# A graph network's edge loops: ring of 24 chunks, destination matrices four at a time, tables ordered by node

## What is computed

```
def _gine(x, src, dst, edge_attr, W1, b1, W2, b2, eW, eb, eps):
    e = edge_attr @ eW + eb
    m = jax.nn.relu(x[src] + e)
    agg = jax.ops.segment_sum(m, dst, num_segments=N)
    h = (1.0 + eps) * x + agg
    return jax.nn.relu(h @ W1 + b1) @ W2 + b2
...
h_all = jnp.einsum('nf,rof->rno', x, W).reshape(r, n, h, d)
h_src = h_all[edge_type, src]
h_dst = h_all[edge_type, dst]
scores = jnp.einsum('ehd,hd->eh', h_src, attn_src) + jnp.einsum('ehd,hd->eh', h_dst, attn_dst)
scores = jnp.where(scores > 0, scores, NEG_SLOPE * scores)
amax = jnp.maximum(jax.ops.segment_max(scores, dst, num_segments=n), 0.0)
w = jnp.exp(scores - amax[dst])
w = w / (jax.ops.segment_sum(w, dst, num_segments=n) + 1e-12)[dst]
out = jax.ops.segment_sum(h_src * w[..., None], dst, num_segments=n)
```

## Time and profile before

| what | value |
|---|---|
| time, median of 3 runs | 4963.34 us (4953.61 to 4967.11) |
| the profiled execution's own time, its span | 5003.4 us, 5001.7 us |
| granted TensorE clock, mean | 0.765 |
| message passes, by windows | 428 to 434 us each, four |
| between passes (layer network, normalisation) | some 70 us each |
| scores stage, attention pass | 500 us, 418 us |
| the rest after attention | 1539 us |

### The profile page before, as it was taken

How to read it: one execution, slowest core, us unless ns; L and a number is a source line. 1 busy time by engine, 2 the same in 40 slices (tenths; PEclk the granted TensorE clock), 3 DMA queues, 4 the chain that set the end, 5 groups by cost and what they waited for, 6 DMA issues and landing times. The chain is left out here.

```text
span 5001.7 us, 66979 instructions
## 1 busy us (share of the span) xinstructions
PE 2986.3 (60%) x16584; PEld 2451.0 (49%) x16585; DVE 2257.8 (45%) x6573; ACT 909.3 (18%) x2422; POOL 2091.8 (42%) x2246
## 2 busy tenths in 40 slices
PE   4566656665666566624366533554677937948392
PEld 3455545554555455514345421222666836947382
DVE  7655555554555455553322235666125441134213
ACT  1122222221222122201011101111120012310020
POOL 4355555556555655553454555663110011020212
PEclk8777877877778787766677755776788968979596
DMA  6522222222223222304221101222766718956494
GB/s 175 184 83 82 70 65 82 82 74 60 82 81 74 62 82 82 77 17 165 49 53 44 44 2 55 85 86 63 242 227 226 239 70 281 329 172 215 142 337 140
DMA packets 394658, 597.59 MB, mean 119 GB/s; under 512 B 105798, under 2 KB 279160, under 8 KB 394104
## 3 DMA queue, kind: packets, MB, share of 16 engines
q1 hardware_dynamic: 274744, 357.76, 21.9%
q0 software_dynamic: 97088, 214.27, 15.5%
q10 hardware_dynamic: 22656, 23.54, 1.4%
HBM read 499.63 MB, written 95.75 MB: 119 GB/s over the span
## 5 line engine op out<-in xcount | busy, mean ns | idle before, releaser
L790 POOL DMA_INDIRECT gine_got<-gine_table,src x1056 | 999.8, 947 | 769.9 <-ACT gine_msg L899 413.6
L886 PE MATMUL gine_p_sum<-gine_hot,gine_msg 128*128 128x128 f32 x4224 | 901.1, 350 | 609.7 <-DVE gine_hot L916 283.5
L886 PEld LDWEIGHTS gine_p_sum<-gine_hot,gine_msg 128*128 128x128 f32 x4224 | 760.2, 253 | 751.7 <-ACT gine_msg L899 538.0
L920 DVE TENSOR_TENSOR gine_got<-gine_got,gine_p_edge 128x256 f32<-128x256 f32 x1056 | 436.6, 413 | 669.1 <-remote 281.5
L899 ACT ACTIVATE gine_msg<-gine_got 128x256 f32<-128x256 f32 x1056 | 439.9, 417 | 1301.2 <-DVE gine_got L920 799.3
L927 DVE TENSOR_TENSOR stack_acc<-stack_acc,gine_p_sum 128x256 f32 x1056 | 434.7, 412 | 2.6
L480 POOL DMA_INDIRECT adjacency<-value,place x264 | 289.2, 1095 | 223.2 <-issue 77.1
L877 PE MATMUL gine_p_edge<-gine_w_a,attrs_t 128*128 128x256 bf16 x1056 | 351.7, 333 | 45.8 <-issue 45.8
L878 PE MATMUL gine_p_edge<-gine_w_b,attrs_t 128*128 128x256 bf16 x1056 | 350.3, 332 | 0.0
L916 DVE TENSOR_SCALAR gine_hot<-iota_free,dst 128x128 f32<-128x128 f32 x1056 | 310.6, 294 | 86.3 <-issue 42.7
L1366 PE MATMUL ffn_p_h<-ffn_xt,ffn_w 128*128 128x128 f32 x2864 | 345.9, 279 | 1.6 <-DMA ffn_w<-in_L_ffn_w 0.9
(11 more groups left out here) (402 smaller groups left out, 3537.6 us busy)
## 6 DMA issues: line engine op xcount, KB each, us to landing
gcn_a<-adjacency SPq DMA_DIRECT2D x270, 320.0 KB, 3.7
ffn_w<-in_L_ffn_W SPq DMA_DIRECT2D x74, 1024.0 KB
ffn_w<-in_L_ffn_w SPq DMA_DIRECT2D x60, 1024.0 KB, 6.3
ffn_w<-in_L_ffn_w SPq DMA_DIRECT2D x90, 512.0 KB
adjacency<-zero_row ACTq DMA_DIRECT2D x3, 7200.0 KB, 43.9
gine_got<-gine_table,src POOLq DMA_INDIRECT x1056
h_table<-score_rows SPq DMA_DIRECT2D x15, 1024.0 KB
adjacency<-zero_row SPq DMA_DIRECT2D x1, 7200.0 KB, 28.0
```

Of the source, the lines that this page charges most:

```text
L790: pool.indirect_dma_start(got[:, u, :], None, table, bass.IndirectOffsetOnAxis(ap=rows[:, c:c + 1], axis=0)).then_inc(gathered[u], 16)
L886: ins = nc.tensor.matmul(p_sum[u % 4][:, half * P:(half + 1) * P], msg[:, u % U, half * P:(half + 1) * P], hot[:, u % U, :], start=True, s ...
L920: nc.vector.tensor_tensor(got[:, u, :], got[:, u, :], p_edge[u % 4][:, 0:D], ALU.add).then_inc(summed, 1)
```

## The change

- `RING = 24` slots of `got` instead of 12. In the message passes the relu works in place in `got`, in attention the multiply and the tail copy too (the slot is 265 wide there), and `msg` is gone. A gather waits for the aggregation of chunk c-24.
- `HOTS = 12` destination matrices, made four at a time by one `tensor_tensor` of 128x512 (`destinations`).
- PE, ScalarE and VectorE are written out over all 264 chunks: waits compare with constants and slices are fixed. The tile register stays (`Tiles`, two banks of 12 registers, one load per 12 chunks). SP's raises are gone.
- The tables' rows are ordered `src * R + etype`: `src_table` is written by one DMA with 256 B pieces, a tile of `h_table` with 8 KB in one piece per partition where it was 8 pieces of 1 KB.

```diff
-            nc.vector.scalar_tensor_tensor(g.hrow[:, some], g.etype[:, some], float(NP), g.src[:, some], ALU.mult, ALU.add)
+            nc.vector.scalar_tensor_tensor(g.hrow[:, some], g.src[:, some], float(R), g.etype[:, some], ALU.mult, ALU.add)
...
+class Tiles:
+    def load(self, c):
+        if c % U == 0:
+            b = c // U % 2
+            self.eng.load(self.registers[b], self.g.chunk_tile[0:1, c:c + U])
+            self.now[b] = [self.eng.snap(r, min_val=0, max_val=T - 1) for r in self.registers[b]]
+def gather_rows(nc, pool, rows, table, got, gathered, used):
+    for c in range(EC):
+        if c >= RING:
+            pool.wait_ge(used, c - RING + 1)
+        pool.indirect_dma_start(got[:, c % RING, :], None, table,
+                                bass.IndirectOffsetOnAxis(ap=rows[:, c:c + 1], axis=0)).then_inc(gathered[c % RING], 16)
+def destinations(nc, v, g, hot, c, agg_done, hot_ready):
+    if c % G == 0:
+        if c >= HOTS:
+            v.wait_ge(agg_done, c + G - HOTS)
+        a = c % HOTS
+        nc.vector.tensor_tensor(hot[:, a:a + G, :], g.iota_free[:, :].unsqueeze(1).to_broadcast([P, G, P]),
+                                g.dst[:, c:c + G].unsqueeze(2).to_broadcast([P, G, P]), ALU.is_equal).then_inc(hot_ready, 1)
...
-            gather_loop(nc, pool, g.src, table, got, gathered, msg_ready)
+            gather_rows(nc, pool, g.src, table, got, gathered, agg_done)
...
+            for c in range(EC + 3):
+                if c < EC:
+                    if c >= 4:
+                        pe.wait_ge(summed, c - 3)
+                    nc.tensor.matmul(p_edge[c % 4][:, 0:D], g.attrs_t[:, c, :], w_a[:, :], start=True, stop=False)
+                    nc.tensor.matmul(p_edge[c % 4][:, 0:D], g.attrs_t[:, c, :], w_b[:, :], start=False, stop=True).then_inc(edge_done, 1)
+                if c >= 3:
+                    d = c - 3
+                    pe.wait_ge(hot_ready, d // G + 1)
+                    if d >= 4:
+                        pe.wait_ge(added, d - 3)
+                    pe.wait_ge(msg_ready, d + 1)
+                    for half in range(2):
+                        ins = nc.tensor.matmul(p_sum[d % 4][:, half * P:(half + 1) * P], got[:, d % RING, half * P:(half + 1) * P],
+                                               hot[:, d % HOTS, :], start=True, stop=True)
+                    ins.then_inc(agg_done, 1)
...
-                    act.wait_ge(agg_done, i * U + (u + 1))
-                    act.wait_ge(summed, i * U + (u + 1 + U))
-                    nc.scalar.activation(msg[:, u, :], got[:, u, :], ACT.Relu).then_inc(msg_ready, 1)
+            for c in range(EC):
+                act.wait_ge(summed, c + 1)
+                nc.scalar.activation(got[:, c % RING, :], got[:, c % RING, :], ACT.Relu).then_inc(msg_ready, 1)
...
+            tiles = Tiles(v, g, ph.name)
+            for c in range(EC + LAG):
+                if c < EC:
+                    tiles.load(c)
+                    destinations(nc, v, g, hot, c, agg_done, hot_ready)
+                    v.wait_ge(edge_done, c + 1)
+                    v.wait_ge(gathered[c % RING], 16 * (c // RING + 1))
+                    nc.vector.tensor_tensor(got[:, c % RING, :], got[:, c % RING, :], p_edge[c % 4][:, 0:D], ALU.add).then_inc(summed, 1)
+                if c >= LAG:
+                    d = c - LAG
+                    if d:
+                        v.wait_ge(added, d)
+                    v.wait_ge(agg_done, d + 1)
+                    a = acc[:, tiles.of(d), :, :].rearrange("p a h n -> p (a h n)")
+                    nc.vector.tensor_tensor(a, a, p_sum[d % 4][:, 0:D], ALU.add).then_inc(added, 1)
+            v.drain()
...
-            for r in range(R):
-                sp.dma_start(src_table[r * NP:(r + 1) * NP, :].rearrange("(t p) h -> p t h", p=P), scores[:, :, r, :])\
-                    .then_inc(scores_written, 16)
+            sp.dma_start(src_table.rearrange("(t p r) h -> p t (r h)", p=P, r=R), scores[:, :, :, :].rearrange("p t r h -> p t (r h)"))\
+                .then_inc(scores_written, 16)
...
-            h_view = h_table.rearrange("(r t p) f -> t p r f", r=R, p=P)
+            h_view = h_table.rearrange("(t p r) f -> t p (r f)", r=R, p=P)
```

More of the change, by code:

```diff
@@ L30 @@
 LAG = 4
+RING = 24
+HOTS = 12
 LN_EPS = 1e-5
-assert EP * EJ == E and EC * P >= E + T * (P - 1) and EC % U == 0 and U % G == 0
+assert EP * EJ == E and EC * P >= E + T * (P - 1) and EC % U == 0 and U % G == 0 and EC % RING == 0
 class Phase:
@@ L791, in gather_loop @@
                                 bass.IndirectOffsetOnAxis(ap=rows[:, c:c + 1], axis=0)).then_inc(gathered[u], 16)
-def add_loop(nc, v, g, ph, each, add):
-    registers = [v.alloc_register(f"{ph.name}_tile{u}") for u in range(U)]
-    def tail(i):
-        last = [v.snap(r, min_val=0, max_val=T - 1) for r in registers[U - LAG:]]
-        return lambda n: add(i, n - LAG, last[n])
-    def one_pass(i):
-        left = tail(i) if not isinstance(i, int) else None
-        for u in range(U):
-            each(i, u)
-            if u < LAG and left:
-                left(u)
-            if u == LAG - 1:
-                tiles = tiles_of(v, g, registers, i)
-            if u >= LAG:
-                add(i, u - LAG, tiles[u - LAG])
-    one_pass(0)
-    with v.Fori(1, EC // U) as i:
-        one_pass(i)
-    left = tail(EC // U)
-    for n in range(LAG):
-        left(n)
-    v.drain()
@@ L823, in lagged, with __init__, of @@
-def lagged(eng, ahead, behind, lag):
-    def one_pass(i):
-        for u in range(U):
-            ahead(i, u)
-            if u >= lag or not isinstance(i, int):
-                behind(i, u - lag)
-    one_pass(0)
-    with eng.Fori(1, EC // U) as i:
-        one_pass(i)
-    for u in range(lag):
-        behind(EC // U, u - lag)
+class Tiles:
+    def __init__(self, eng, g, name):
+        self.eng, self.g, self.now = eng, g, [None, None]
+        self.registers = [[eng.alloc_register(f"{name}_tile{b}_{u}") for u in range(U)] for b in range(2)]
+    def load(self, c):
[3 more added lines that the diff above has]
+            self.now[b] = [self.eng.snap(r, min_val=0, max_val=T - 1) for r in self.registers[b]]
+    def of(self, c):
+        return bass.ds(self.now[c // U % 2][c % U], 1)
@@ L851, in gine_edges @@
         loaded, split = ph.sem("loaded"), ph.sem("split")
-        gathered = [ph.sem(f"gathered{u}") for u in range(U)]
+        gathered = [ph.sem(f"gathered{u}") for u in range(RING)]
         edge_done, summed, msg_ready, hot_ready = ph.sem("edge_done"), ph.sem("summed"), ph.sem("msg_ready"), ph.sem("hot_ready")
@@ L2237, in _ @@
         @block.scalar
         def _(act):
-            with act.Fori(0, EC // U) as i:
-                for u in range(U):
-                    act.wait_ge(agg_done, i * U + (u + 1))
-                    act.sem_inc(turn, 1)
-                    nc.scalar.copy(msg[:, u, D:WIDE], weights[:, bass.ds(i * U + u, 1), :].rearrange("p a w -> p (a w)"))\
-                        .then_inc(tail_ready, 1)
+            for c in range(EC):
+                if c >= RING:
+                    act.wait_ge(agg_done, c - RING + 1)
+                nc.scalar.copy(got[:, c % RING, D:WIDE], weights[:, c, :]).then_inc(tail_ready, 1)
```

103 lines of the change are left out of this document (34 added, 69 removed).

## The result

The changed kernel takes 4825.9 us (median of 4 runs, 4816.7 to 4828.0) where the kernel before took 4959.2 beside it: a ratio of 0.9726, interval 0.9706 to 0.9747, so 133 us less. The forecast was 4750.

What follows compares the result with a forecast made beforehand. The prediction took a hand-over as the bound, PE's completions seen late while POOL gathers. Ring 176, attention 44 and tables 6 us sum to 226, 4963 to 4737, set at 4750 us for pass starts; range 4490 to 5040 us.

Steps and rivals of the forecast that it cites:

- What bounds the kernel: Message passes and attention: no engine full, bound by a hand-over, PE's completions being seen late while POOL gathers.
- Ring and messages in place: Four message passes: POOL restarts 1.15 us earlier in each of 38 cycles, 44 us a pass, 176 us (bounds 0 to 400).
- POOL is the pacemaker where it runs, and its waits are the whole rest: Third message pass: 264 gathers at 1.25 us are 330 us, plus 101.7 us of POOL's waits, the 430 measured.
- Straight-line code: PE, ScalarE and VectorE written out over 264 chunks: 0 us, upper end of the cost 130 us in all.
- 44 us forecast: Attention: same ring and constant waits for register waits save half of POOL's 88 us over its pace (ends 0 and 88).
- Matrices: Four destination matrices per instruction save 33 us of VectorE's time a pass, counted as 0; up to 165 us if VectorE bound.
- The port: VectorE and GpSimd share a port pair: each of 66 merged matrices a pass could hold a gather, up to 45 us.
- the slow rival: (c), slower: POOL runs twice as long without a pause and starves the others; 5090 us, chance 0.20.
- Tables: Before the first score gather: one source-table write for eight saves 6 us (0 to 10); the wide table nothing.
- (b): Balance: ring depth only lengthens cycles, only cheaper matrices help; 4880 us, chance 0.12, or no gain, 4960 us, 0.09.
- (a): POOL at its own pace: the lag comes from loops and short ring, and goes; 4530 us, chance 0.22.
- (c): With 24 slots the others starve while POOL gathers, 26 us a pass more; 5090 us, chance 0.20.

Runs made afterwards that it cites:

- the separate buffer: Against the changed kernel with 12 slots: in message passes the relu writes a separate 12-slot buffer and gathers wait for the relu of c-12; 4906.3 us, ratio 0.9782.

## Why the prediction was near, and where it was wrong

The range held and the sign was right, but part of the agreement is luck: one term was too large, one gain and one loss were missed.

**What bounds the kernel.** Right, and now shown: PE's completions are late while POOL gathers (no wait for an edge matmul left without gathers, 4 short ones of 2.2 us in all with as many rows from SyncE). What in POOL's gathering does it stays open. Neither bytes nor traffic do.

**Ring and messages in place, 176 us (44 a pass).** POOL's pauses did shrink as worked out: gathers of the second pass that start more than 1.7 us after the one before hold 90 us over the pace of 1.25 before, and 49 us after, 41 less. But the cause was mostly another. Straight-line code alone brings that sum to 64. What is left to the term itself is the step from the separate buffer to the ring of 12: 76 to 91 us when it is taken back from the ring of 12, and some 60 when it comes on top of straight-line code, a third to a half of the forecast. And depth, which I had counted on the gain's side, costs: rings of 8 and 12 keep the same pace, and the drain of 24 slots takes 55 us back, so that little of the term is left in the changed kernel. The step that failed is "POOL is the pacemaker where it runs, and its waits are the whole rest": a pass ends with the last add, not with the last gather, and with 24 slots that add is done 19 to 21 us after the last gather begins (8.8 with 12).

**Straight-line code, 0 us.** The largest miss, 114 us. I took its cover from POOL's own straight loop and from the first twelve chunks, which stall although they are written out. They show that the stall remains, not that it remains as long; and they run beside ScalarE's loop, which has register waits from the first chunk on. My row for the cost was there: 2.4 us before VectorE's accumulator add in attention, after register waits, and I counted it in attention alone (44 us forecast; 26 between the profiles, of which some 4 are the chip's, and 25 of the 26 are there with straight-line code alone). The Trainium skill (Runtime: NRT & Kernel Launch, Instruction fetch mechanics) names the break of the prefetch by taken branches as one reason for full unrolling. Its result is what came. Its reason isn't seen where the trace can show it, since behind the jump back VectorE idles 0.14 us once in 12 chunks, 3 us a pass. Register waits come in each chunk, but 520 plain instructions more cost only 5 us a pass, and no run has a loop with constant waits. What in the loops costs the 20 us a pass stays open.

**Matrices, 0 us.** Right within what could be told: 11 us at most of the 165 that I had as the upper end. The port, which I had put into the slow rival at up to 45 us a pass and seen no sign of in the rows of before, is there: gathers that begin beside a merged matrix are longer, 6 us a pass. That agrees with the Trainium skill (SBUF — State Buffer, Who interferes with whom), by which a VectorE instruction with two SBUF inputs contends with a GpSimd instruction that reads SBUF (the gather's row numbers lie there), and the issue order decides who blocks. Its size is a seventh of the 45 us: a gather that is already running isn't stretched, and one that begins inside a matrix is stretched by half of what the matrix has left (1142 for 948 ns, with 410 ns left on average). The sign was in the trace of before, since the earlier trace rows has attention's gathers at 981 ns for 947: the multiply there has two SBUF inputs, and of the 62 gathers that begin inside one, 49 are over 1 us, of the other 202 two.

**Tables, 6 us.** 9 to 13.

**The rivals.** (b) was right on the depth: slots don't change the pace under gathering. (a) would have needed the stall to end. (c)'s starving is seen at the start of a pass (9.06 us for a chunk), but it costs no pace after that. Along one path the parts are 114 us (code), 82 (in place, matrices and tables together, with the ring of 12) and -55 (depth), 141 us for the 133 measured; the kernel before took 4967.8 us beside the kernels of the path and 4959.2 beside the changed one. Of the 82 some 10 are the tables' and 5 to 11 the matrices'.

The best kernel run here is the changed one with a ring of 12: 0.9604 of before, against 0.9726.

## What to carry to other kernels

A ring deeper than the landing of its transfers needs doesn't smooth a stall that recurs, and it can be paid for as drain at the end of every pass (24 slots for 12: 55 us; 12 for 8: nothing): try the depth downwards as well. A hardware loop whose waits compare with registers, on engines that hand over to each other in every step, can cost time that the profile books as waiting for others (114 us of 4968 here, 2.3%); write one such loop out before explaining the waits. When one engine's completions come late, silence the suspected neighbour in one run and keep its traffic in another, before building depth against it.

## What the runs showed of the hardware

While POOL issued indirect gathers (0.95 us each, every 1.25 us), VectorE waited up to 10.5 us for edge matmuls recorded as done (331 waits over 0.5 us in four passes, 604 us in all), with the raise of their semaphore recorded just before it went on; what VectorE and ScalarE handed over in the same passes was taken up within 0.04 and 0.21 us. With the same number of rows from SyncE's queue (141 GB/s) this was gone, and from the first edge term's add to the last add a pass took 235 us for 395. Halving the gathered bytes changed nothing (4827.3 us for 4825.9). When PE worked on pairs of chunks its records also stood still for up to 1.03 us inside the aggregation shown, where they otherwise follow each other at 0.11 us; in the changed kernel no step there is over 0.35 us. A gather that began while VectorE ran an instruction with two inputs from SBUF was longer (1142 ns on average and up to 1.47 us beside 128x512 elements, for 948); one that was running already was not (948 ns), and beside 128x128 with one such input they stayed at 947. Two chips differed by 1% on the same kernel (4968 and 5013.6 us), most of it in stretches where POOL gathers.
